# A two-layer graph network kernel: value products of two head pairs in one step, and row norms turned by rounded full-width products

## The chip, the cores and the metric

The kernel runs on one core of a Trainium2 chip. The metric is the device time of one execution in microseconds. Before the change it was 335.44 us, the median of 3 runs (334.61 to 335.58). All times of the profile come from one further, profiled execution of 335.22 us.

## The reference

625 nodes with 512 features each, 10,000 edges of 3 types. Layer 0 sums messages over the edges, and layer 1 is an attention with 8 heads of 64 over the same edges. Each layer normalises its input, clips it at zero, and its output is added to its input. The part around the change:

```
qkv = x @ W_qkv.T + b_qkv;  Q, K, V = split(qkv), each [nodes, 8, 64]
scores = einsum('ehd,ehd->eh', Q[receivers], K[senders]) / sqrt(64)
ex     = exp(scores - segment_max(scores)[receivers])
att    = ex / segment_sum(ex, receivers)[receivers]
msg    = segment_sum(att[:, :, None] * V[senders], receivers)
out    = msg.reshape(nodes, 512) @ W_ff.T + b_ff
```

## The kernel before

The kernel doesn't gather edges. In a first stage it counts them: one-hot rows made by VectorE and multiplied by TensorE give a dense table `adjT` of how many edges of each type run between two nodes. Layer 0 is then a set of dense products with that table (`z`, `gemm` units). For layer 1 the logarithm of the counts becomes a mask that is added to dense scores of 640 x 640 nodes (625, padded to five tiles of 128), so that the softmax over all nodes equals the one over the edges.

The attention is the last stage. It runs over five tiles of 128 receiving nodes and, in each, over 8 heads. Its steps are:

- `score` (TensorE, L1324): scores of one head of one tile, 128 x 640, in four products of 320 columns of rounded 32-bit numbers (F32R), a high and a low part of the keys. They go to two pairs of PSUM banks in turn, so a score step waits for the maximum of the step two before.
- `smax` (VectorE, L1019): adds the mask, copies to `s_sb` and takes the maximum.
- `exp` (ScalarE, L673): exponential into `p_sb`, with the row sums in `denom`.
- `turn` (TensorE, L1335): four transposes of 128 x 128 of `p_sb` into bank 5 or 6. `fill` copies them to `pT`, on ScalarE (L680) for even numbers and on VectorE (L1029) for odd ones. A `turn` waits for the `fill` two before.
- `pv` (TensorE, L1349): values times probabilities for one pair of heads, in bank 4: five blocks of nodes for each of two heads. A head has 64 values, so each product fills 64 partitions only, the even head the lower and the odd head the upper ones. The numbers are plain 32-bit, and each product appears in the trace as two instructions.
- `norm` (VectorE, L1036 and L1038): one over the row sums, [128 nodes, 8 heads], once a tile, when its last `exp` is done.
- `rb` (TensorE, L1359): the sums are per receiving node, but in bank 4 the node is the column. So the norm of each head is multiplied, broadcast to 64 columns, with the identity, which gives in bank 7 a 64 x 128 block with the norm of each column; eight products, again 64 partitions each. ScalarE copies bank 7 to `r_sb` (L687).
- `msg` (VectorE, L1048, then ScalarE L694 and GpSimd L497): bank 4 times `r_sb`, split in a high and a low part.
- `ff` (TensorE, L1369): the output product, four steps of three products of 512 columns, in bank 7; `out` (VectorE, L1055) adds the input, and a DMA stores the tile.

All engines run these steps in one order, the list `attention`: each step has a time in units of one head, from a few constants (`TURN`, `PV`, `RB`, `FF`), and the list is sorted by it. Each engine takes its own kinds of steps from it in that order; semaphores keep them together. In the steady state a `pv` step comes every two heads, `rb` comes between two `turn` and `score` steps of the next tile.

Of the kernel before, what the change touches and what calls it, by code (L numbers as in the profile page):

```python
# [26 lines left out]
F32 = mybir.dt.float32  # L27
F32R = mybir.dt.float32r
# [3 lines left out]
I32 = mybir.dt.int32  # L32
# [4 lines left out]
P = 128  # L37
# [5 lines left out]
def gnn_kernel(nc, x_d, src_d, dst_d, etype_d, ntype_d, wrel_d, brel_d, wself_d, bself_d,  # L43
# [28 lines left out]
    with ExitStack() as ctx:  # L72
        def sb(name, shape, dt):
            return ctx.enter_context(nc.sbuf_tensor(name, shape, dt))

        def sem(name):
            return ctx.enter_context(nc.semaphore(name))


        xs = sb("xs", [P, NT, D], F32)  # L80
        ident = sb("ident", [P, P], F32)
        ident16 = sb("ident16", [P, P], F16)
        bhl = sb("bhl", [BROWS, D], F32R)
        bv_rows = sb("bv_rows", [P, D], F32)
# [19 lines left out]
        tile_off = sb("tile_off", [1, 2, 8], F32)  # L104
        tile_off_i = sb("tile_off_i", [1, 8], I32)
        place_u = sb("place_u", [P, NT], U32)
        bounds = sb("bounds", [1, 3, 32], I32)
        bounds_f = sb("bounds_f", [1, 4, 32], F32)
        stats = sb("stats", [P, NT, 6], F32)
        mv = sb("mv", [P, 2, NT, 2], F32)  # L110
        rstd = sb("rstd", [P, 2, NT, 2], F32)
# [4 lines left out]
        neg_max = sb("neg_max", [P, NT, H], F32)  # L116
        denom = sb("denom", [P, NT, H], F32)
        recip = sb("recip", [P, 2, H], F32)
        norm = sb("norm", [P, 2, H], F32)


        Z_BYTES = 2 * KD * NP * 4
# [5 lines left out]
        def place(name, offset, shape, dt):  # L128
            return nc.alloc_sbuf_tensor_at(name, shape, dt, offset=arena0 + offset)
# [28 lines left out]
        edges_f = place("edges_f", o_r4 + 58752, [EC, 3, EL], F32)  # L158
        below = place("below", o_r4 + 60256, [P, P], F32)
        ones = place("ones", o_r4 + 60768, [P, P], F32)  # L160
        tile_iota = place("tile_iota", o_r4 + 61280, [P, 8], F32)
        full = place("full", o_r4 + 61312, [P, NT], F32)
        above = place("above", o_r4 + 61344, [P, T, NT], F32)
# [21 lines left out]
        sorted_d = nc.dram_tensor("sorted_rows", [SP, D], F32, kind="Internal").ap()  # L185
        self_d = nc.dram_tensor("self_rows", [SP, D], F32, kind="Internal").ap()

        banks = ctx.enter_context(nc.psum_tensor("banks", [P, 8, 512], F32))


        s_fill = sem("s_fill")
        s_edges = sem("s_edges")
        s_nodes = sem("s_nodes")
        s_x = sem("s_x")
# [130 lines left out]
        for f, at in enumerate(turn_at):  # L325
            placed += [(at, "turn", f), (at + 0.1, "fill", f)]
        pv_at = [turn_at[((2 * n + 2) * NT - 1) // 4] + PV for n in range(NT * KD)]
        placed += [(at, "pv", n) for n, at in enumerate(pv_at)]
        for it in range(NT):
            msg_at = max(pv_at[(it + 1) * KD - 1], it * H + RB) + 0.1  # L330
            placed += [((it + 1) * H, "norm", it), (it * H + RB, "rb", it)]
# [73 lines left out]
        def _(pool):  # L405
# [17 lines left out]
            nc.gpsimd.memset(edge_keys[:], 0.0).then_inc(s_fill, 1)  # L423
            pool.wait_ge(s_fill, 4)
            nc.gpsimd.tensor_copy(ident16[:], ident[:]).then_inc(s_fill, 1)
            nc.gpsimd.memset(zero_rows[:], 0.0).then_inc(s_fill, 1)
            nc.gpsimd.memset(ones[:], 1.0).then_inc(s_fill, 1)
            nc.gpsimd.memset(type_base[:], 0.0).then_inc(s_fill, 1)
# [269 lines left out]
        def _(dve):  # L698
# [311 lines left out]
            for step in attention:  # L1010
                kind, n = step
                if kind == "smax":
                    it, h = divmod(n, H)
                    dve.wait_ge(s_sc, n + 1)
                    dve.wait_ge(s_mask, 2 * (it + 1))
                    if n >= NS:
                        dve.wait_ge(s_exp, n - NS + 1)
                    c = 2 * (n % 2)
                    nc.vector.tensor_tensor_reduce(  # L1019
                        s_sb[:, n % NS, :].rearrange("p (a j) -> p a j", a=2), banks[:, c:c + 2, 0:HALF],  # L1020
                        mask_add[:, it, :].rearrange("p (a j) -> p a j", a=2), 1.0, 3.0e38, ALU.add, ALU.min,
                        neg_max[:, it, h:h + 1]).then_inc(s_smax, 1)
                    if n == 1:
                        split_q(KD - 1)
                elif kind == "fill" and n % 2 == 1:
                    dve.wait_ge(s_tr, n + 1)
                    if 4 * n + 3 >= NT * H:
                        dve.wait_ge(s_pv, (4 * n + 3 - NT * H) // (2 * NT) + 1)
                    nc.vector.tensor_copy(pT[:, 4 * n % (NT * H):4 * n % (NT * H) + 4, :],  # L1029
                                          banks[:, 5 + n % 2, :].rearrange("p (s i) -> p s i", s=4)  # L1030
                                          ).then_inc(s_ptd, 1)
                elif kind == "norm":
                    dve.wait_ge(s_exp, H * (n + 1))
                    if n >= 2:
                        dve.wait_ge(s_rb, n - 1)
                    chain(nc.vector.reciprocal(recip[:, n % 2, :], denom[:, n, :]))  # L1036

                    nc.vector.scalar_tensor_tensor(out=norm[:, n % 2, :], in0=neg_max[:, n, :], scalar=BIG / 2,  # L1038
                                                   in1=recip[:, n % 2, :], op0=ALU.is_lt, op1=ALU.mult
                                                   ).then_inc(s_norm, 1)  # L1040
                elif kind == "msg":
                    it, a = divmod(n, KD)
                    if a == 0:
                        dve.wait_ge(s_pv, KD * (it + 1))
                        dve.wait_ge(s_rsb, it + 1)
                    if it >= 1:
                        dve.wait_ge(s_mlo, n + 1 - KD)
                    nc.vector.tensor_tensor(msg_f[:, a], banks[:, 4, a * P:(a + 1) * P], r_sb[:, a],  # L1048
                                            ALU.mult).then_inc(s_msg, 1)
                elif kind == "out":  # L1050
                    dve.wait_ge(s_ff, n + 1)
                    dve.wait_ge(s_xb, n + 1)
                    if n >= 2:
                        dve.wait_ge(s_out[n % 2], 16 * (n // 2))
                    nc.vector.tensor_tensor(ybuf[:, n % 2, :], banks[:, 7, :], xs[:, n, :], ALU.add  # L1055
                                            ).then_inc(s_fin, 1)
# [3 lines left out]
        def _(pe):  # L1060
# [247 lines left out]
            for step in attention:  # L1308
# [18 lines left out]
                elif kind == "turn":  # L1327
                    pe.wait_ge(s_exp, (4 * n + 3) // NT + 1)
                    if n == 0:
                        pe.wait_ge(s_ufree, len(ring))  # L1330
                    if n >= 2:
                        pe.wait_ge(s_pta if n % 2 == 0 else s_ptd, n // 2)
                    for i in range(4):
                        h, jt = divmod(4 * n + i, NT)
                        ins = nc.tensor.transpose(banks[:, 5 + n % 2, i * P:(i + 1) * P],  # L1335
                                                  p_sb[:, h % NPR, jt * P:(jt + 1) * P], ident[:])
                    ins.then_inc(s_tr, 1)
                elif kind == "pv":
                    it, a = divmod(n, KD)
                    f = ((2 * n + 2) * NT - 1) // 4  # L1340
                    pe.wait_ge(s_pta, (f + 2) // 2)
                    pe.wait_ge(s_ptd, (f + 1) // 2)
                    if a == 0 and it >= 1:
                        pe.wait_ge(s_msg, KD * it)
                    for jt in range(NT):
                        for hh in range(2):
                            s = ((2 * n + hh) * NT + jt) % (NT * H)
                            h = 2 * a + hh
                            ins = mm(banks[64 * hh:64 * hh + 64, 4, a * P:(a + 1) * P],  # L1349
                                     v_sb[:, jt, h * DK:(h + 1) * DK], pT[:, s, :],  # L1350
                                     start=(jt == 0), stop=(jt == NT - 1), skip_group_check=True)
                    ins.then_inc(s_pv, 1)
                elif kind == "rb":
                    pe.wait_ge(s_norm, n + 1)
                    if n >= 1:
                        pe.wait_ge(s_fin, n)
                    for h in range(H):
                        me = 64 * (h % 2)
                        ins = mm(banks[me:me + 64, 7, h // 2 * P:(h // 2 + 1) * P],  # L1359
                                 norm[:, n % 2, h:h + 1].broadcast_to([P, DK]), ident[:],  # L1360
                                 start=(h < 2), stop=True, skip_group_check=True)
                    ins.then_inc(s_rb, 1)
                elif kind == "ff":
                    it, kt = divmod(n, KD)
                    pe.wait_ge(s_mlo, n + 1)
                    if kt == 0:
                        pe.wait_ge(s_rsb, it + 1)
                    for k, (pl, pw) in enumerate(PASSES):
                        ins = mm(banks[:, 7, :], msgT[:, it % 2, pl, kt, :], wffT[:, pw, kt, :],  # L1369
                                 start=(kt == 0 and k == 0), stop=(kt == KD - 1 and k == len(PASSES) - 1),  # L1370
                                 skip_group_check=True)
                    if kt == KD - 1:
                        ins.then_inc(s_ff, 1)
# [31 lines left out]
```

## Time and profile before

| | |
|---|---|
| median of 3 runs | 335.44 us (334.61 to 335.58) |
| profiled execution | 335.22 us, of which span 333.5 us |
| TensorE busy | 302.0 us (91%) |
| VectorE busy | 201.2 us (60%) |
| ScalarE busy | 143.0 us (43%) |
| GpSimd busy | 71.7 us (22%) |
| granted TensorE clock, mean | 0.974 |

The span is the time from the first to the last instruction; the execution has 1.7 us around it. The attention runs from about 234 us to the end. An engine that is busy for most of a stretch isn't shown to be the bound by that alone: the chain of waits, followed back from the last instruction, says which engine's work the end hangs on.

### The profile page before, as it was taken

Reading aid. Unit: us, or ns where it says so; the run is one execution under the profiler, and the core shown is the slowest. Engines: PE = TensorE matmul, PEld = TensorE weight load, DVE = VectorE, ACT = ScalarE, POOL = GpSimd, SP = SyncE. Lnnn points to the kernel's source line nnn. Section 1 sums busy time; section 2 is a strip of 40 time slices with the busy share of each in tenths; the row PEclk is TensorE's granted clock in tenths of the full one; section 3 lists DMA queues with packets and bytes.
Section 4 is the critical chain, followed back from the end, with each engine's and each line's share of the span. In section 5 each row is a group of like instructions: output and inputs, shape, how many; then the busy total and the mean of one; then the engine's idle time right before and its main releaser. Section 6 shows DMA issues by size and latency. Waiting matters only on the chain.

```text
span 333.5 us, 5488 instructions
## 1 busy us (share of the span) xinstructions
PE 302.0 (91%) x2006; PEld 228.6 (69%) x2006; DVE 201.2 (60%) x471; ACT 143.0 (43%) x282; POOL 71.7 (22%) x97
## 2 busy tenths in 40 slices
PE   2757699996699999999999999999799999999994
PEld 2512344442356778868788789999688888888883
DVE  5999944557794324434446962784976556565721
ACT  1155213236032332253342451677876466565721
POOL 6059500005840004470001330320001002020202
PEclk9999789998599999999999999999999999999999
DMA  5852894110740000003520000000000000000000
GB/s 173 281 186 100 267 392 154 38 64 33 253 152 13 2 1 3 2 2 128 149 103 2 0 0 3 0 2 1 0 2 0 34 2 2 32 2 33 1 33 28
DMA packets 10970, 22.29 MB, mean 67 GB/s; under 512 B 950, under 2 KB 966, under 8 KB 10938
## 3 DMA queue, kind: packets, MB, share of 16 engines
q1 hardware_dynamic: 8772, 16.80, 14.5%
q0 software_dynamic: 800, 2.62, 2.2%
q10 hardware_dynamic: 1366, 2.45, 2.1%
q8 instruction: 20, 0.33, 0.4%
q14 instruction: 12, 0.10, 0.1%
HBM read 15.60 MB, written 6.26 MB: 66 GB/s over the span
## 4 chain that ended last, share of the span: by engine, by line
PE 78%; DVE 14%; issue 2%; ACT 2%; DMA 2%; POOL 0%; DVEq 0%
PE banks L1260 13%; PE banks L1246 8%; PE banks L1206 8%; PE banks L1151 8%; PE banks L1349 7%; PE banks L1335 7%; PE banks L1324 7%; DVE key_hot L833 6%; PE banks L1099 6%; PE banks L1369 5%; DVE row_hot L840 3%; PE banks L1192 2%; DMA raw<-in_L_gnn_W_qkv_dram 2%; PE banks L1359 2%; PE banks L1236 1%
## 5 line engine op out<-in xcount | busy, mean ns | idle before, releaser
L1099 PE MATMUL banks<-key_hot,row_hot 128*128 128x480 f16 x120 | 35.8, 438 | 14.7 <-DVE key_hot L833 12.3
L1019 DVE CUSTOM_DVE_ANT_0 s_sb<-banks,mask_add 128x640 f32<-128x640 f32 x40 | 32.6, 822 | 22.2 <-PE banks L1324 22.1
L833 DVE TENSOR_SCALAR key_hot<-iota,picked 128x480 f16<-128x480 f16 x120 | 41.2, 410 | 0.0
L673 ACT ACTIVATE p_sb<-s_sb,neg_max 128x640 f32<-128x640 f32 x40 | 32.9, 823 | 17.3 <-DVE neg_max L1019 17.3
L1099 PEld LDWEIGHTS banks<-key_hot,row_hot 128*128 128x128 f16 x120 | 12.7, 108 | 36.8 <-DVE key_hot L833 15.7
L1206 PE MATMUL banks<-adjT,h 128*128 128x320 f16 x240 | 33.8, 299 | 0.6 <-DVE zT_even L892 0.6
L840 DVE TENSOR_TENSOR row_hot<-iota,picked_row 128x768 f16<-128x768 f16 x20 | 21.9, 1097 | 18.9 <-PE banks L1099 18.9
L1206 PEld LDWEIGHTS banks<-adjT,h 128*128 128x128 f16 x240 | 23.2, 98 | 10.4 <-DVE zT_even L892 1.2
L1335 PE MATMUL banks<-ident,p_sb 128*128 128x128 f32 x200 | 29.6, 275 | 0.2 <-ACT pT L680 0.2
L1260 PE MATMUL banks<-w_hl,zT_even 128*128 128x512 f32 x120 | 29.2, 394 | 0.0
L497 POOL TENSOR_TENSOR msgT<-msg_f,msgT 128x128 fp32r<-128x128 f32 x20 | 8.6, 460 | 95.7 <-ACT msgT L694 95.7
L1324 PE MATMUL banks<-k_hi,q_st 128*128 128x320 f32 x80 | 27.1, 348 | 2.0 <-DVE neg_max L1019 2.0
L1246 PE MATMUL banks<-h2T,wqkvT 128*128 128x320 f32 x192 | 28.3, 309 | 0.0
L1246 PEld LDWEIGHTS banks<-h2T,wqkvT 128*128 128x128 f32 x192 | 28.2, 188 | 0.1
L530 ACT ACTIVATE adjT<-banks 128x480 f16<-128x480 f32 x20 | 11.3, 570 | 37.2 <-PE banks L1099 37.1
L1151 PE MATMUL banks<-w_self,hsT 128*128 x56 | 26.7, 622 | 0.0
L1349 PE MATMUL banks<-pT,v_sb 128*64 128x128 f32 x400 | 26.0, 277 | 0.0
L1335 PEld LDWEIGHTS banks<-ident,p_sb 128*128 128x128 f32 x200 | 23.5, 141 | 3.0 <-issue 1.9
L1260 PEld LDWEIGHTS banks<-w_hl,zT_even 128*128 128x128 f32 x120 | 22.3, 188 | 4.4
L1349 PEld LDWEIGHTS banks<-pT,v_sb 128*64 128x64 f32 x400 | 21.5, 137 | 4.0 <-issue 3.8
L1324 PE MATMUL banks<-k_lo,q_st 128*128 128x320 f32 x80 | 24.0, 309 | 0.0
L446 POOL TENSOR_TENSOR w_hl<-raw,w_hl 128x512 fp32r<-128x512 f32 x12 | 15.0, 1284 | 41.5 <-ACT w_hl L521 41.5
(176 smaller groups left out, 473.3 us busy)
## 6 DMA issues: line engine op xcount, KB each, us to landing
w_self<-in_L_gnn_W_self_dram SPq DMA_DIRECT2D x3, 1024.0 KB, 9.4
raw<-in_L_gnn_W_rel_dram SPq DMA_DIRECT2D x3, 1024.0 KB, 14.6
raw<-in_L_gnn_W_qkv_dram SPq DMA_DIRECT2D x3, 1024.0 KB, 5.2
sorted_rows<-zero_rows ACTq DMA_DIRECT2D x1, 1792.0 KB, 10.9
self_rows<-hs SPq DMA_DIRECT2D x7, 256.0 KB, 2.0
hs<-sorted_rows SPq DMA_DIRECT2D x1, 1280.0 KB, 7.2
xs<-in_x_dram SPq DMA_DIRECT2D x1, 1024.0 KB
raw<-in_L_gnn_W_ff_dram SPq DMA_DIRECT2D x1, 1024.0 KB, 5.4
```

Of the source, the lines that this page charges most:

```text
L673: nc.scalar.activation(p_sb[:, n % NPR, :], s_sb[:, n % NS, :], ACT.Exp, scale=-1.0, bias=neg_max[:, it, h:h + 1], accum_out=denom[:, it, ...
L833: return nc.vector.tensor_scalar(to_key, iota[:], float(KEYS * w), key, ALU.add, ALU.is_equal)
L840: nc.vector.tensor_tensor(row_hot[:, par], iota[:, 0:P].unsqueeze(1).broadcast_to([P, G, P]), picked_row[:, w * G:(w + 1) * G].unsqueeze(2 ...
L1019: nc.vector.tensor_tensor_reduce(s_sb[:, n % NS, :].rearrange("p (a j) -> p a j", a=2), banks[:, c:c + 2, 0:HALF], mask_add[:, it, :].rear ...
L1099: mm(banks[:, w % 2, 0:KEYS], row_hot[:, w % 2, k, :], key_hot[:, w % 2, k, :], start=(k == 0), stop=True, skip_group_check=True).then_inc ...
L1151: ins = mm(pipe_bank(u), hsT[:, t % 4, kt, :], w_self[:, bass.ds(offsets[t] + kt * D, D)], start=(kt == 0), stop=(kt == KD - 1))
L1206: ins = mm(b[:, 0:HALF], h16[:, p, jt, feats], adj[:, jt, r, cols], start=(start and n == 0), stop=(stop and n == len(pick) - 1), skip_gro ...
L1246: ins = mm(b[:, 0:HALF], wqkvT[:, pw, kt, o:o + P], h2T[:, ph, kt, half * HALF:(half + 1) * HALF], start=(n == 0), stop=(n == 3 * KD - 1))
L1260: ins = mm(to, lhs[:, pl, kt, it * P:(it + 1) * P], weights[:, pw, kt, c0:c0 + cn], start=(start and n == 0), stop=(n == 3 * KD - 1), skip ...
L1324: ins = mm(banks[:, 2 * (n % 2) + half, 0:HALF], q_st[:, h, it * P:(it + 1) * P], k[:, h, cols], start=(p == 0), stop=(p == 1))
L1335: ins = nc.tensor.transpose(banks[:, 5 + n % 2, i * P:(i + 1) * P], p_sb[:, h % NPR, jt * P:(jt + 1) * P], ident[:])
L1349: ins = mm(banks[64 * hh:64 * hh + 64, 4, a * P:(a + 1) * P], v_sb[:, jt, h * DK:(h + 1) * DK], pT[:, s, :], start=(jt == 0), stop=(jt == ...
```

## The change

Two edits in the attention, and what they need.

The first sets the time of both `pv` steps of two neighbouring head pairs to that of the later one. The sort then puts them next to each other.

The second makes `rb` full width. VectorE now spreads the norm of each head over 64 columns itself, rounds this to F32R (`norm_hl[:, 0]`), and subtracts what was rounded from the exact one to have the rest (`norm_hl[:, 1]`). TensorE multiplies high and low parts of two heads together, 128 x 128, by an identity in F32R, eight products a tile, into the same places of bank 7. `norm_hl` has one buffer, so a `norm` step waits for the `rb` of the tile before. GpSimd makes the F32R identity at the start, and the small tables `bounds` are placed elsewhere.

```diff
+        ident_r = sb("ident_r", [P, P], F32R)
...
-        norm = sb("norm", [P, 2, H], F32)
+        norm = sb("norm", [P, H], F32)
...
+        norm_hl = place("norm_hl", o_r4 + 35328, [P, 2, H, DK], F32R)
...
-        placed += [(at, "pv", n) for n, at in enumerate(pv_at)]
+        placed += [(pv_at[n // 2 * 2 + 1], "pv", n) for n in range(NT * KD)]
...
             nc.gpsimd.tensor_copy(ident16[:], ident[:]).then_inc(s_fill, 1)
+            nc.gpsimd.tensor_copy(ident_r[:], ident[:]).then_inc(s_ident, 1)
...
-                    if n >= 2:
-                        dve.wait_ge(s_rb, n - 1)
+                    if n >= 1:
+                        dve.wait_ge(s_rb, n)
                     chain(nc.vector.reciprocal(recip[:, n % 2, :], denom[:, n, :]))
 
-                    nc.vector.scalar_tensor_tensor(out=norm[:, n % 2, :], in0=neg_max[:, n, :], scalar=BIG / 2,
-                                                   in1=recip[:, n % 2, :], op0=ALU.is_lt, op1=ALU.mult
-                                                   ).then_inc(s_norm, 1)
+                    chain(nc.vector.scalar_tensor_tensor(out=norm[:], in0=neg_max[:, n, :], scalar=BIG / 2,
+                                                         in1=recip[:, n % 2, :], op0=ALU.is_lt, op1=ALU.mult))
+                    spread = norm[:].unsqueeze(2).broadcast_to([P, H, DK])
+                    chain(nc.vector.tensor_copy(norm_hl[:, 0], spread))
+                    nc.vector.tensor_tensor(norm_hl[:, 1], spread, norm_hl[:, 0].bitcast(F32),
+                                            ALU.subtract).then_inc(s_norm, 1)
...
-                    for h in range(H):
-                        me = 64 * (h % 2)
-                        ins = mm(banks[me:me + 64, 7, h // 2 * P:(h // 2 + 1) * P],
-                                 norm[:, n % 2, h:h + 1].broadcast_to([P, DK]), ident[:],
-                                 start=(h < 2), stop=True, skip_group_check=True)
+                    if n == 0:
+                        pe.wait_ge(s_ident, 1)
+                    for a in range(KD):
+                        for p in range(2):
+                            ins = mm(banks[:, 7, a * P:(a + 1) * P],
+                                     norm_hl[:, p, 2 * a:2 * a + 2, :].rearrange("p h d -> p (h d)"),
+                                     ident_r[:], start=(a == 0 and p == 0), stop=(p == 1), skip_group_check=True)
```

TensorE, tile 0, from the transposes in front of the first `pv` step, before the change. L1335 are transposes, L1324 scores, L1349 value products:

```order
L1335 MATMUL banks<-ident,p_sb 128x128 x4
L1349 MATMUL banks<-pT,v_sb 64x128 x10
L1324 MATMUL banks<-k_hi,q_st 128x320
L1324 MATMUL banks<-k_lo,q_st 128x320
L1324 MATMUL banks<-k_hi,q_st 128x320
L1324 MATMUL banks<-k_lo,q_st 128x320
L1335 MATMUL banks<-ident,p_sb 128x128 x8
L1324 MATMUL banks<-k_hi,q_st 128x320
L1324 MATMUL banks<-k_lo,q_st 128x320
L1324 MATMUL banks<-k_hi,q_st 128x320
L1324 MATMUL banks<-k_lo,q_st 128x320
L1349 MATMUL banks<-pT,v_sb 64x128 x10
```

The same place after it (L1343 are the transposes, L1332 the scores, L1357 the value products):

```order
L1343 MATMUL banks<-ident,p_sb 128x128 x4
L1332 MATMUL banks<-k_hi,q_st 128x320
L1332 MATMUL banks<-k_lo,q_st 128x320
L1332 MATMUL banks<-k_hi,q_st 128x320
L1332 MATMUL banks<-k_lo,q_st 128x320
L1343 MATMUL banks<-ident,p_sb 128x128 x8
L1332 MATMUL banks<-k_hi,q_st 128x320
L1332 MATMUL banks<-k_lo,q_st 128x320
L1332 MATMUL banks<-k_hi,q_st 128x320
L1332 MATMUL banks<-k_lo,q_st 128x320
L1357 MATMUL banks<-pT,v_sb 64x128 x20
L1343 MATMUL banks<-ident,p_sb 128x128 x4
```

The first value step, which stood between transposes 5 and score 8, now stands behind score 9, joined with the second.

TensorE around the norm step of tile 3 (L1359), before:

```order
L1324 MATMUL banks<-k_lo,q_st 128x320
L1335 MATMUL banks<-ident,p_sb 128x128 x4
L1359 MATMUL banks<-ident,norm 64x128 x8
L1324 MATMUL banks<-k_hi,q_st 128x320
L1324 MATMUL banks<-k_lo,q_st 128x320
L1324 MATMUL banks<-k_hi,q_st 128x320
L1324 MATMUL banks<-k_lo,q_st 128x320
L1335 MATMUL banks<-ident,p_sb 128x128 x4
L1349 MATMUL banks<-pT,v_sb 64x128 x10
L1324 MATMUL banks<-k_hi,q_st 128x320
```

After (the norm step is L1369):

```order
L1332 MATMUL banks<-k_lo,q_st 128x320
L1343 MATMUL banks<-ident,p_sb 128x128 x4
L1369 MATMUL banks<-ident_r,norm_hl 128x128 x8
L1332 MATMUL banks<-k_hi,q_st 128x320
L1332 MATMUL banks<-k_lo,q_st 128x320
L1332 MATMUL banks<-k_hi,q_st 128x320
L1332 MATMUL banks<-k_lo,q_st 128x320
L1343 MATMUL banks<-ident,p_sb 128x128 x4
L1332 MATMUL banks<-k_hi,q_st 128x320
```

The value step that followed one score later has gone from here to the next pair, and the norm step has products of 128 rows of output.

VectorE, the norm step of tile 0 with the copy of transposes before it and the next maximum behind it, before:

```order
L1029 COPY pT<-banks 128x512
L1036 RECIPROCAL recip<-denom 128x8
L1038 SCALAR_TENSOR_TENSOR norm<-neg_max,recip 128x8
L1019 ISA s_sb,neg_max<-banks,mask_add 128x640
L1019 ISA neg_max 128x1
L1029 COPY pT<-banks 128x512
```

After:

```order
L1034 COPY pT<-banks 128x512
L1041 RECIPROCAL recip<-denom 128x8
L1043 SCALAR_TENSOR_TENSOR norm<-neg_max,recip 128x8
L1046 CAST norm_hl<-norm 128x512
L1047 TENSOR_TENSOR norm_hl<-norm,norm_hl 128x512
L1024 ISA s_sb,neg_max<-banks,mask_add 128x640
L1024 ISA neg_max 128x1
L1034 COPY pT<-banks 128x512
```

Two operations of 128 x 512 have come in ahead of the next maximum.

## Rows read from the trace of the kernel before

**Rows 1.** Page, chain that ended last: share of the span by engine.

```profile
PE 78%; DVE 14%; issue 2%; ACT 2%; DMA 2%; POOL 0%; DVEq 0%
```

**Rows 2.** Stretches, the attention: length; busy PE, PEld, DVE, ACT, POOL; clock; DMA.

```profile
240.00:326.00 86.00, 85.75 (x856) 74.61 (x854) 51.17 (x126) 49.62 (x117) 6.87 (x16) 1.00 0.04 14
```

**Rows 3.** Chain of waits in order of time: start us, us, what.

```profile
242.55 0.44 PE banks L1335 x4
...
245.89 0.59 PE banks L1324 x4
246.48 1.24 PE banks L1349 x20
247.72 0.59 PE banks L1335 x4
...
250.36 0.78 PE banks L1324 x4
...
258.95 0.70 PE banks L1369 x3
...
260.89 0.91 PE banks L1369 x3
...
268.08 1.02 PE banks L1359 x16
269.11 0.79 PE banks L1324 x4
...
323.57 2.21 PE banks L1349 x40
```

**Rows 4.** VectorE's groups by shape: count, busy us, mean ns, idle before.

```profile
L936 DVE CAST k_hi<-qk_f 64x640 fp32r<-64x640 f32 x8 | 5.3, 665 | 4.9 <-ACT qk_f L588 4.7
...
L999 DVE SCALAR_TENSOR_TENSOR xs<-self_sum,xs 128x512 f32<-128x512 f32 x5 | 3.5, 692 | 0.2
...
L946 DVE CAST k_lo<-k_lo 64x640 fp32r<-64x640 f32 x2 | 1.0, 490 | 0.1
...
L1038 DVE SCALAR_TENSOR_TENSOR norm<-neg_max,recip 128x8 f32<-128x8 f32 x5 | 0.8, 167 | 0.2
```

**Rows 5.** Timeline of TensorE's products behind value step 2: start us, us.

```profile
252.75 0.41 PE L1324 MATMUL banks<-k_hi,q_st 128*128 128x320 f32 x1
253.00 0.31 PE L1324 MATMUL banks<-k_lo,q_st 128*128 128x320 f32 x1
253.15 0.31 PE L1324 MATMUL banks<-k_hi,q_st 128*128 128x320 f32 x1
```

**Rows 6.** Timeline of TensorE's weight loads there, the second load.

```profile
252.85 0.19 PEld L1324 LDWEIGHTS banks<-k_lo,q_st 128*128 128x128 f32 x1
```

**Rows 7.** Timeline of VectorE around the norm steps of tiles 0, 1 and 4.

```profile
243.34 0.69 DVE L1029 COPY pT<-banks 128x512 f32<-128x512 f32 x1
244.46 0.20 DVE L1036 RECIPROCAL recip<-denom 128x8 f32<-128x8 f32 x1 [0.44 <-ACT p_sb L673]
...
245.05 0.82 DVE L1019 CUSTOM_DVE_ANT_0 s_sb<-banks,mask_add 128x640 f32<-128x640 f32 x1 [0.18 <-PE banks L1324]
...
260.78 0.17 DVE L1038 SCALAR_TENSOR_TENSOR norm<-neg_max,recip 128x8 f32<-128x8 f32 x1
262.42 0.82 DVE L1019 CUSTOM_DVE_ANT_0 s_sb<-banks,mask_add 128x640 f32<-128x640 f32 x1 [1.47 <-PE banks L1324]
...
319.88 0.69 DVE L1055 TENSOR_TENSOR ybuf<-banks,xs 128x512 f32<-128x512 f32 x1 [2.71 <-PE banks L1369]
```

**Rows 8.** Timeline of the start: GpSimd, ScalarE and TensorE around the identities.

```profile
3.91 0.34 POOL L425 CAST ident<-ident 128x128 f16<-128x128 f32 x1
...
6.22 0.20 ACT L536 ACTIVATE warm<-eps_c 128x1 f32<-128x1 f32 x1 [0.31 <-POOL sel L442]
...
8.45 0.47 ACTq L538 DMA_DIRECT2D sorted_rows<-zero_rows  x1
...
12.40 0.74 PEld L1105 LDWEIGHTS banks<-type_mask,below 128*128 128x128 f32 x2 [0.25 <-issue]
```

More of the change, by code:

```diff
@@ L106, in gnn_kernel @@
         place_u = sb("place_u", [P, NT], U32)
-        bounds = sb("bounds", [1, 3, 32], I32)
-        bounds_f = sb("bounds_f", [1, 4, 32], F32)
         stats = sb("stats", [P, NT, 6], F32)
@@ L160, in gnn_kernel @@
         ones = place("ones", o_r4 + 60768, [P, P], F32)
+        bounds = place("bounds", o_r4 + 64000, [1, 3, 32], I32)
+        bounds_f = place("bounds_f", o_r4 + 64384, [1, 4, 32], F32)
         tile_iota = place("tile_iota", o_r4 + 61280, [P, 8], F32)
@@ L186, in gnn_kernel @@
         self_d = nc.dram_tensor("self_rows", [SP, D], F32, kind="Internal").ap()
+        norm_hl = place("norm_hl", o_r4 + 35328, [P, 2, H, DK], F32R)
         banks = ctx.enter_context(nc.psum_tensor("banks", [P, 8, 512], F32))
         s_fill = sem("s_fill")
+        s_ident = sem("s_ident")
         s_edges = sem("s_edges")
```

## The prediction

> **What bounds the kernel now.** I read the chain of waits by engine first: 78% of the span hangs on TensorE, 14% on VectorE, nearly all of the latter in the adjacency stage at the start [rows 1]. Then the table by stretches: from 240 to 326 us TensorE is busy for 85.75 of 86.00 us, at a granted clock of 1.00 (2.4 GHz), while VectorE has 51 us and ScalarE 50 us of work [rows 2]. The edit changes nothing that is computed outside this stretch, which is the attention: its time is the sum of TensorE's steps. So I read the steps themselves off the chain of waits, where each piece runs from the end of the piece before to its own end [rows 3].
>
> Those rows show a cost that no instruction carries. Twenty value products (a step of one head pair, output on 64 partitions) take 1.24 us, but forty in one row take 2.21 us, so twenty cost 1.105 and about 0.14 is paid on the way in. What comes next is also longer than usual: a score step takes 0.78 us straight behind them and 0.59 elsewhere, a step of four transposes 0.59 against 0.44, an output step 0.91 against 0.70 [rows 3]. So every visit to the 64-wide form costs 0.14 us going in and 0.15 (transposes), 0.19 (scores) or 0.21 (output) coming out. The norm product is such a visit too: sixteen instructions in 1.02 us, which is 16 x 0.0553 = 0.885 plus 0.14 [rows 3].
>
> **The change, part by part.** *Pairing the value steps.* Before, a tile has four value steps and one norm step, each between full-width steps; for tiles 0 to 3 that makes 5 visits each, and for tile 4 there are 3, because the last norm step and two value steps already stand together: 23 visits. After, the value steps stand in twos and the norm step is full width: 2 visits per tile, 10 in all. 13 visits go. Nine of them were left into a score step (value steps 0, 2, 6, 10, 14 and norm steps 0 to 3), four into an output step (4, 8, 12, 16). 13 x 0.14 + 9 x 0.19 + 4 x 0.21 = 1.82 + 1.71 + 0.84 = 4.4 us off, all on TensorE, in a stretch where TensorE sets the time.
>
> *The norm products.* Out go, five times, sixteen instructions worth 0.885 us. In come eight rounded products of 128 x 128, with 128 columns moving. No row has a rounded product with so few columns, so I bound it. Above full speed it can't go: four score products of 320 columns take 0.59, 0.147 each, and three output products of 512 columns 0.70, 0.233 each [rows 3]; the line through both (0.45 ns a column) gives 0.061 us at 128 columns. But the weights have to be loaded, too. The first score product behind a visit is followed by the second after 0.25 us, the second by the third after 0.15 [rows 5]; the load in between is issued as soon as the first is through, 0.10 after it [rows 6]: a load of rounded weights that hides behind nothing costs 0.10 us. With 320 columns it hides; with 128 it doesn't fit under 0.061, so one product each 0.10 to 0.11 us is what I take, the same as one transpose now (0.44 / 4 [rows 3]). Eight make 0.87 us: no gain, no loss. Below: 0.061 each if the loads are quicker in a row, 8 x 0.061 = 0.49, 5 x 0.40 = 2.0 us less. Above: if moving and loading don't overlap, 0.16 to 0.17; if a short rounded product runs like an unrounded one, which takes two instructions of 0.109 (0.44 / 4 again, four transposes with 128 columns), 0.22; if its load isn't hidden either, 0.32.
>
> A rule that speaks against the cheap case: the Trainium skill, "TensorE: Matmul & The Clock Gate", Part 3, "The mechanism", says that a weight load overlaps with products in flight only where the row group differs. All of these products use all rows, so by the rule each would pay load and product one after the other. This trace doesn't agree for 320 columns: there the spacing is 0.147 us although every product has its own load of 0.10 [rows 5, 6]. For 128 columns no row decides, so it is a rival below.
>
> *Norms on VectorE.* Before, reciprocal and norm take 0.4 us with their link (0.20 and 0.167 [rows 4, 7]). In come a copy that spreads 8 values to 512 and rounds them, and a subtraction of 128 x 512. The copy's nearest rows are rounding casts of 64 x 640, 0.665 us and 0.490 [rows 4]; for 512 of 640 columns that is 0.39 to 0.53 us, with a broadcast read perhaps up to the 0.69 us of a 128 x 512 operation. The subtraction is of the size of L999, 0.69 us [rows 4]. I take 0.55 + 0.69 and two links of 0.03: 1.3 us more, five times (1.1 to 1.5). What hides it: in tile 1 VectorE waits 1.47 us behind the norm for the next scores, in tiles 2 and 3 the same, in tile 4 2.71 us for the output step [rows 7]. TensorE comes there earlier now by one value step and its visit, about 1.4 us, so up to 1.3 us of VectorE's work becomes late against it in tiles 1 to 3; but the maximum behind the norm is asked for only by the score step two later, behind output steps 2 and 3 of that tile, transposes and the value pair, over 4 us of TensorE's work. Nothing comes of it. In tile 0 the next score maximum begins 0.2 us behind the norm [rows 7], so it is late by 1.1 us, at about 246.1 instead of 245.05, and done at 247. Behind it on VectorE stand the copy of transposes 7 and the next maximum. TensorE asks for maximum 8 in score step 10, which now stands behind score 9, two value steps and transposes 8: at least 244.8 + 0.59 + 2.3 + 0.6 = 248.3. Slack 1.3 us: nothing. In the last tile the output sum behind the norm waits for TensorE longer than 1.3 us in any case. ScalarE's copy of the norms stays where it is, on an engine with 50 us of work in 86.
>
> *What is late next.* Where a value step went away, it had covered something. Transposes 7 wait for VectorE's copy of transposes 5, which began at 243.34 and ended at 244.03 [rows 7]. TensorE used to come there at about 245.4, 0.44 before the score step at 245.89 [rows 3]; now score 8, transposes 6 and transposes 7 follow the end of transposes 5 at 242.99 (242.55 + 0.44 [rows 3]) directly, so it arrives at about 243.7 and waits for 0.3 us. In later tiles the same place holds the norm step between score steps, and copies and exponentials are ahead by 0.2 us or more. Once, +0.3 us. The slots for transposed values: the first to be overwritten belongs to transposes 10, two transposes behind the moved pair; nothing.
>
> *At the start.* GpSimd copies the identity once more, about the 0.34 us of its fp16 copy, so that its last fill ends near 6.5 us instead of 6.2. ScalarE's next work behind it is the issue at 8.45, TensorE's first use 12.40 [rows 8]. Nothing. The bounds only lie elsewhere.
>
> **The sum.** -4.4 + 0.0 + 0.3 = -4.1 us. The profiled execution took 335.22 us (333.5 of span and 1.7 around it), so 331.1; the median of the runs is 0.2 higher, so 331.3.
>
> **The rivals.**
> Loads in a row are quicker (0.061 each): -6.1 us, 329.3. For it: the fit through 320 and 512 columns. Against: the 0.10 us of the bare load. Chance 0.06.
> Load and product don't overlap at 128 columns (0.165 each): eight take 1.32, 0.44 more than before, five times 2.2: 333.5. For it: a bare load is longer than the product, and no row shows how they share the array then. This is also what the skill's rule above would do. Chance 0.14.
> The gain is given back: short rounded products cost what unrounded ones cost (0.22). Eight take 1.76, 0.88 more, five times 4.4: the visits' saving is eaten, 335.7. For it: nothing in the trace shows that rounding is cheap below 320 columns, and 128-column products here all have 0.109 an instruction. Against: rounded products are one instruction, not two. Chance 0.20.
> Slower: the same, with the load of rounded weights bare each time (0.32): 2.56 a tile, 8.4 us more in all, minus 4.1: 339.7. It decides from 0.25 us a product on, where 5 x (2.0 - 0.885) = 5.6 us outweighs the saving by over 0.3%. Against: a product that long should hide a load of 0.10. Chance 0.08, with every other way to lose more than 1 us.
> That the pairs don't join (visits still paid inside a pair) I leave out: the last two value steps, already adjacent, run at 2.21 for forty [rows 3].
>
> **How the numbers follow.** My forecast has 0.52 and its own range is 330.2 to 332.1 (0.09 to 0.12 a product, waits of 0 to 0.6). Within 0.3% (1 us, what a measurement of this kernel can tell from no change) lies the third rival alone. Faster: 0.52 + 0.06 + 0.14 = 0.72; same 0.20; slower 0.08. The range for 8 in 10 goes from 330.2 to 335.8 and leaves out the first and the last rival, 0.14.
>
> **What would show it.** The chain after should have 2.3 us for each forty value products, ten of them, no value step of twenty, and score steps of 0.59 everywhere, behind the norm step too. The norm step should have eight instructions and take 0.87 us: 0.49 would be the first rival, 1.3 the second, 1.8 the third, 2.6 the fourth. VectorE should show 1.2 to 1.3 us for the two new operations and less idle time before the maxima, with TensorE still at about 81.5 us busy between 240 and 322. If TensorE shows idle time of over 1 us in the attention, a wait that I priced at 0.3 took the place of the visits and the forecast is wrong.

## The result and the profile after

The changed kernel takes 331.38 us (median of 4 runs, 331.32 to 331.60) against 335.51 us before: a ratio of 0.988 (95% interval 0.985 to 0.990), 4.1 us less. The forecast was 331.3.

The profiled execution took 331.60 us with a span of 329.9 us. That is only 3.6 us less than the one of before, because in it the attention began 0.5 us later. The stage itself is better measured by itself, from the start of the first score maximum to the start of the last output sum, on VectorE's timeline. Columns are start us, us and the instruction. Before:

```profile
233.50 0.82 DVE L1019 CUSTOM_DVE_ANT_0 s_sb<-banks,mask_add 128x640 f32<-128x640 f32 x1 [1.28 <-PE banks L1324]
...
330.11 0.69 DVE L1055 TENSOR_TENSOR ybuf<-banks,xs 128x512 f32<-128x512 f32 x1 [3.43 <-PE banks L1369]
```

After:

```profile
234.00 0.83 DVE L1024 CUSTOM_DVE_ANT_0 s_sb<-banks,mask_add 128x640 f32<-128x640 f32 x1 [1.28 <-PE banks L1332]
...
326.50 0.69 DVE L1063 TENSOR_TENSOR ybuf<-banks,xs 128x512 f32<-128x512 f32 x1 [3.41 <-PE banks L1379]
```

96.61 us before, 92.50 after: 4.11 us less. Below, "the stage" is this length. A second profile of the changed kernel had 92.49, so I read it to some hundredths, where whole runs tell about 1 us; no other kernel has a second profile.

The chain of waits after, from tile 0 into tile 1 and one period later, in the columns of [rows 3]. L1357 are value products, L1343 transposes, L1332 scores, L1379 output products and L1369 the norm step:

```profile
243.92 0.61 DVE pT L1034
244.54 0.14 issue
244.67 0.63 PE banks L1343 x4
245.31 0.58 PE banks L1332 x4
245.89 2.33 PE banks L1357 x40
248.22 0.59 PE banks L1343 x4
248.81 0.59 PE banks L1332 x4
249.41 0.44 PE banks L1343 x4
249.84 0.84 PE banks L1369 x8
250.68 0.64 PE banks L1332 x4
...
258.79 1.39 PE banks L1379 x6
...
267.57 0.84 PE banks L1369 x8
...
285.29 0.84 PE banks L1369 x8
```

Every value step is a block of forty in 2.33 us (2.36 for the last one, straight behind a norm step). The transposes behind such a block are still longer than their kind (0.59 for 0.44). The norm step takes 0.84 us instead of 1.02, and 0.64 instead of 0.78 for the scores behind it; six output products stand together in 1.39, where one value step used to split them in 0.70 and 0.91 [rows 3]. From one norm step to the next it is 17.72 us (285.29 - 267.57). The first three rows are the new wait: transposes 7 stand behind VectorE's copy of transposes 5, and they take 0.63 us instead of 0.44.

VectorE's norm step of tile 1, timeline, which answers to [rows 7]:

```profile
260.82 0.43 DVE L1046 CAST norm_hl<-norm 128x512 fp32r<-128x512 f32 x1
261.28 0.69 DVE L1047 TENSOR_TENSOR norm_hl<-norm,norm_hl 128x512 fp32r<-128x512 f32 x1
261.89 0.82 DVE L1024 CUSTOM_DVE_ANT_0 s_sb<-banks,mask_add 128x640 f32<-128x640 f32 x1
```

The 1.47 us of idle time ahead of the next maximum are gone: VectorE goes straight on. The stretches, for [rows 2], 86 us that begin 4 us earlier, as the stage now ends earlier:

```profile
236.00:322.00 86.00, 84.32 (x836) 77.58 (x834) 60.05 (x143) 53.56 (x126) 6.88 (x16) 1.00 0.04 14
```

VectorE has 60 us of work in it. TensorE has 1.7 us of idle time, of which 1.5 lie ahead of 240 us, where the kernel before has as much; from 240 to 322 us it is busy for 81.84 of 82.00 us, at the full clock.

### The profile page after: what moved, and what is told of

Its sections match the earlier page's. It is cut to its first block, busy times and chain, and to the rows that moved or that the text cites. A ratio compares the mean times of both kernels' runs of the same rounds, so it can differ in the third digit from the quotient of the medians.

```text
span 329.9 us, 5421 instructions
## 1 busy us (share of the span) xinstructions
PE 295.4 (90%) x1966; PEld 228.2 (69%) x1966; DVE 208.2 (63%) x481; ACT 143.7 (44%) x282; POOL 67.6 (21%) x98
## 4 chain that ended last, share of the span: by engine, by line
PE 77%; DVE 16%; ACT 3%; issue 2%; DMA 1%; POOL 0%; DVEq 0%
PE banks L1268 14%; PE banks L1214 9%; PE banks L1254 9%; PE banks L1159 7%; PE banks L1357 7%; PE banks L1343 6%; DVE key_hot L838 6%; PE banks L1332 6%; PE banks L1107 5%; PE banks L1379 4%; DVE row_hot L845 2%; PE banks L1244 2%; PE banks L1200 2%; PE banks L1369 1%; PE banks L1231 1%
## 5 line engine op out<-in xcount | busy, mean ns | idle before, releaser
L1107 PE MATMUL banks<-key_hot,row_hot 128*128 128x480 f16 x120 | 34.9, 427 | 16.8 <-DVE key_hot L838 13.0
L838 DVE TENSOR_SCALAR key_hot<-iota,picked 128x480 f16<-128x480 f16 x120 | 42.2, 417 | 0.0
L1343 PE MATMUL banks<-ident,p_sb 128*128 128x128 f32 x200 | 29.8, 275 | 0.3 <-ACT pT L685 0.2
L1332 PE MATMUL banks<-k_hi,q_st 128*128 128x320 f32 x80 | 26.8, 344 | 2.0 <-DVE neg_max L1024 2.0
L1343 PEld LDWEIGHTS banks<-ident,p_sb 128*128 128x128 f32 x200 | 23.5, 141 | 3.3 <-issue 2.3
L1159 PE MATMUL banks<-w_self,hsT 128*128 x56 | 25.5, 599 | 0.0
L1332 PE MATMUL banks<-k_lo,q_st 128*128 128x320 f32 x80 | 24.1, 309 | 0.0
L1357 PE MATMUL banks<-pT,v_sb 128*64 128x128 f32 x400 | 24.0, 275 | 0.0
L1357 PEld LDWEIGHTS banks<-pT,v_sb 128*64 128x64 f32 x400 | 21.6, 137 | 1.8 <-issue 1.7
```

Source lines behind the costliest of these rows:

```text
L838: return nc.vector.tensor_scalar(to_key, iota[:], float(KEYS * w), key, ALU.add, ALU.is_equal)
L1107: mm(banks[:, w % 2, 0:KEYS], row_hot[:, w % 2, k, :], key_hot[:, w % 2, k, :], start=(k == 0), stop=True, skip_group_check=True).then_inc ...
L1159: ins = mm(pipe_bank(u), hsT[:, t % 4, kt, :], w_self[:, bass.ds(offsets[t] + kt * D, D)], start=(kt == 0), stop=(kt == KD - 1))
L1332: ins = mm(banks[:, 2 * (n % 2) + half, 0:HALF], q_st[:, h, it * P:(it + 1) * P], k[:, h, cols], start=(p == 0), stop=(p == 1))
```

## The experiments

The theory: a change between products that fill 64 output partitions and full-width ones costs TensorE time on both sides; the change removes 13 of 23 visits to the narrow form, and the norm step in its new form costs what the old one did. The rivals: that only one of the two edits matters, that the price belongs to plain 32-bit numbers and not to the width, and that relief of other engines gave the time. All stage lengths, each from the same two rows of its kernel's profile. Where the last column says "one execution", there is only the profiled one, and the stage alone is compared:

| kernel | stage us | against the changed kernel | ratio of runs to before (95%) |
|---|---|---|---|
| before | 96.61 | +4.11 | |
| changed, again | 92.49 | -0.01 | 0.989 (0.986 to 0.991) |
| pairs only | 93.68 | +1.18 | 0.991 (0.989 to 0.993) |
| norm step only | 95.24 | +2.74 | 0.998 (0.996 to 0.999) |
| plain full-width norms | 92.54 | +0.04 | 0.988 (0.986 to 0.990) |
| 64 columns moved | 92.50 | 0.00 | one execution |
| 256 columns moved | 92.82 | +0.32 | one execution |
| norm products twice | 96.94 | +4.44 | one execution |
| narrow 16-bit norms | 90.81 | -1.69 | one execution |
| full-width 16-bit norms | 91.07 | -1.43 | 0.984 (0.981 to 0.987) |
| value steps in fours | 94.22 | +1.72 | 0.992 (0.989 to 0.994) |
| more VectorE work | 97.69 | +5.19 | one execution |
| 16-bit norms, later | 90.48 | -2.02 | 0.981 (0.979 to 0.983) |

**The changed kernel again.**

> The changed kernel once more, beside the others on the same chip: 4.1 us faster than before. It is the measure for the other three.

Median 330.51 us beside 334.73 of before: 4.2 us less.

**Pairs only.** The kernel before with

```diff
-        placed += [(at, "pv", n) for n, at in enumerate(pv_at)]
+        placed += [(pv_at[n // 2 * 2 + 1], "pv", n) for n in range(NT * KD)]
```

> The kernel before with the value steps paired and nothing else. Theory (a change between 64-wide and full-width products costs TensorE 0.14 us in and 0.15 to 0.21 us out): 9 visits go, 9 x 0.14 + 5 x 0.19 + 4 x 0.21 = 3.05 us, less one new wait of 0.3 us for the copy of transposes 5: 2.7 us faster than before, with TensorE's chain pieces of 2.33 us for forty value products and the norm steps unchanged at 1.02 and 0.78 behind. Rival (the time came from the norm step's new form, and pairing only moves work): 0 to 1 us faster.

The stage is 2.93 us shorter, the runs' medians 3.0 (331.72 against 334.73). The chain of waits (value products L1349, norm step L1359):

```profile
248.18 0.44 PE banks L1335 x4
248.61 1.02 PE banks L1359 x16
249.64 0.79 PE banks L1324 x4
```

The norm step is as it was, so the rival falls: most of the gain is the pairing's.

**Norm step only.** The changed kernel with that line the other way round.

> The changed kernel with the value steps back in their old places: only the norm step is full width. Theory: 4 visits go, 4 x (0.14 + 0.19) = 1.3 us, and the step itself is 0.84 us instead of 0.885, but 0.06 is lost in the scores behind it: 1.3 us faster than before, and the two parts add up to the whole (2.7 + 1.3 = 4.0). Rival (VectorE's 1.1 us more in every tile needs the room that pairing made): 0 to 0.5 us faster or slower, with new idle time on TensorE before score or transpose steps.

1.37 us shorter; medians 333.94 against 334.73. The medians differ by less than the stage, but the interval of their ratio, 0.2 to 1.5 us, holds it. TensorE has no wait that the kernel before didn't have, so VectorE's extra work fits without the pairing too.

The parts add to 4.30, 0.2 more than the whole. The chains of waits show where: from the norm step of tile 1 to that of tile 2 it is 18.74 us before, 18.01 with pairs only, 18.41 with the norm step only and 17.72 with both, so 1.02 us off where the parts give 1.06. It is much the same in each of the four such stretches, and lies in hundredths: six output products take 1.39 and 1.40 us with both edits, 1.38 and 1.39 with pairs only, and the scores are longer by as little. What makes them longer is open.

**Plain full-width norms.** VectorE spreads the norms exactly, TensorE multiplies them unsplit:

```diff
-                    chain(nc.vector.tensor_copy(norm_hl[:, 0], spread))
-                    nc.vector.tensor_tensor(norm_hl[:, 1], spread, norm_hl[:, 0].bitcast(F32),
-                                            ALU.subtract).then_inc(s_norm, 1)
+                    nc.vector.tensor_copy(norm_f[:], spread).then_inc(s_norm, 1)
...
                     for a in range(KD):
-                        for p in range(2):
-                            ins = mm(banks[:, 7, a * P:(a + 1) * P],
-                                     norm_hl[:, p, 2 * a:2 * a + 2, :].rearrange("p h d -> p (h d)"),
-                                     ident_r[:], start=(a == 0 and p == 0), stop=(p == 1), skip_group_check=True)
+                        ins = mm(banks[:, 7, a * P:(a + 1) * P],
+                                 norm_f[:, 2 * a:2 * a + 2, :].rearrange("p h d -> p (h d)"),
+                                 ident[:], start=(a == 0), stop=True, skip_group_check=True)
```

> The changed kernel with the norm step full width but in plain 32-bit numbers: VectorE spreads the norms exactly, without the low part, and TensorE issues four products (two instructions each) instead of eight rounded ones. Theory (a rounded product of 128 columns is bound by its weight load at 0.105 us, a plain instruction by its 128 columns at 0.109, and the width alone makes the visit): 8 x 0.109 = 0.87 us a step against 0.84 + 0.06 behind it, so the same time as the changed kernel within 0.3 us, with 0.6 us less VectorE work a tile. Rival (visits belong to plain 32-bit products, not to the width): the step and what is behind it show 0.14 and 0.19 again, 4 x 0.33 = 1.3 us slower than the changed kernel.

Chain of waits, the norm step (L1366) of tile 0 and the scores behind it:

```profile
249.14 0.89 PE banks L1366 x8
250.03 0.59 PE banks L1330 x4
```

No visit, though the numbers are the plain 32-bit ones of before: the width makes the price. (The weights of the old norm step were also read as a broadcast, which here they are not; but the value steps have no broadcast and paid the same 0.14 and 0.19.) The step's 0.89 is the changed kernel's 0.84 plus the 0.05 that there come out in the scores. So the split in high and low parts bought nothing; only the full width did. VectorE has one operation of 0.69 us less in each tile here, and the stage is no shorter: that work is hidden in the changed kernel. The medians say the same (330.96 and 330.51).

**64 and 256 columns.** The changed kernel's norm products with `ident_r[:, 0:64]`, and with `ident_r[:].unsqueeze(1).broadcast_to([P, 2, P])` into 256 columns.

> The changed kernel, but its eight norm products move only the first 64 columns of the identity (so only half of the norms are made). Theory (the weight load sets the pace of a short rounded product): spacing stays at 0.105 us, the norm step at about 0.84 us. Rival (2 cycles a column): 0.055 us each, the step 0.45 us.

> The changed kernel, but its norm products move 256 columns (the identity twice, into two neighbouring quarters of the bank, so that the sums are wrong). Theory (weight load of about 0.105 us beside 1 cycle a column): 256 columns take 0.107 to 0.12 us, the step 0.86 to 0.96 us and the score step behind it back at 0.59. Rival (2 cycles a column below some length): 0.21 us each, the step 1.7 us, the execution 4.4 us slower than the changed kernel.

Chain of waits, norm step and scores behind it, with 64 columns:

```profile
249.75 0.81 PE banks L1369 x8
250.56 0.67 PE banks L1332 x4
```

With 256:

```profile
248.70 0.95 PE banks L1369 x8
249.65 0.58 PE banks L1332 x4
```

With what is above 0.59 behind it counted in, a product costs (0.81 + 0.08) / 8 = 0.111 us with 64 columns, (0.84 + 0.05) / 8 = 0.111 with 128 and (0.95 - 0.01) / 8 = 0.118 with 256 (the other tiles have 0.95 to 0.97, up to 0.121). The time doesn't follow the columns; what is left is the weight load. The timeline of the changed kernel's weight loads fits that. Behind the norm step the second load of the scores starts 0.11 us after the first, though the product of the first moves 320 columns:

```profile
250.46 0.19 PEld L1332 LDWEIGHTS banks<-k_hi,q_st 128*128 128x128 f32 x1
250.57 0.19 PEld L1332 LDWEIGHTS banks<-k_lo,q_st 128*128 128x128 f32 x1
```

No run changes the load alone, so another fixed cost of a product of this type isn't excluded. The load would also explain the scores behind the step: their own load hides behind a norm product, and the fewer columns that has, the less it hides (0.08, 0.05, nothing). It would explain as well why the step with 64 columns was 0.03 us under the expected 0.84.

**Twice.** The same products issued again.

> The changed kernel with every norm step's eight products issued twice over. Theory (TensorE sets the time of the attention, and nothing else is near): 5 x 0.84 = 4.2 us more than the changed kernel, all of it in the norm step. Rival (other engines are close behind TensorE, so part of its work is free): clearly less than 4.2 us.

The norm piece is 1.74 us for sixteen, 0.90 more, and the stage 4.44 longer, against 5 x 0.90 = 4.5. All of it counts: TensorE is the bound, and eight products cost 0.90, not 0.84, once nothing of them is moved into the scores. So I don't take relief of another engine for the cause of the gain.

**Narrow 16-bit norms.** The step 64 wide again, with `norm16` and `ident16`.

> The changed kernel with the norm step 64-wide again but in 16-bit numbers (norms rounded to fp16, no low part: eight products of one instruction). Theory (the change of width costs, whatever the numbers): the step is short, but the visit is there: 0.1 to 0.15 us going in beyond its products, and 0.15 to 0.2 us more than 0.59 in the score step behind the norm. Rival (the price belongs to plain 32-bit products): score steps behind it take 0.59 to 0.65 as in the changed kernel.

Chain of waits, tile 1:

```profile
266.43 0.34 PE banks L1366 x8
266.78 0.79 PE banks L1329 x4
```

The scores behind it take 0.79 again, as behind the old narrow step. In the timeline the two products of a pair, one for each half of the partitions, start within 0.01 us of each other, and the pairs follow at 0.056; four pairs of that leave some 0.12 for going in. So 16-bit numbers pay the price of a visit too: it belongs to the width. The stage is shorter all the same, since 0.34 + 0.79 us stand where the changed kernel has 0.84 + 0.64: there is no low part, so there are eight half-width products in place of eight full-width ones, and they are of the quicker type.

**Full-width 16-bit norms**, high and low part in fp16, against the changed kernel:

```diff
-        norm_hl = place("norm_hl", o_r4 + 35328, [P, 2, H, DK], F32R)
+        norm16 = place("norm16", o_r4 + 35328, [P, 2, H, DK], F16)
...
-                                     norm_hl[:, p, 2 * a:2 * a + 2, :].rearrange("p h d -> p (h d)"),
-                                     ident_r[:], start=(a == 0 and p == 0), stop=(p == 1), skip_group_check=True)
+                                     norm16[:, p, 2 * a:2 * a + 2, :].rearrange("p h d -> p (h d)"),
+                                     ident16[:], start=(a == 0 and p == 0), stop=(p == 1), skip_group_check=True)
```

> The changed kernel with the norms in two 16-bit parts (fp16 high and low, and the fp16 identity) instead of two rounded 32-bit parts; still eight full-width products a tile. Theory (a rounded product of 128 columns is paced by its weight load, 0.112 us; the width alone makes the visit): a 16-bit product is paced by its 128 columns, about 0.055 us as in the 64-wide 16-bit step, so the norm step takes 0.45 us instead of 0.84 and the score step behind it stays at 0.59 to 0.65: 5 x 0.4 = 2 us faster than the changed kernel, perhaps 0.1 a tile less where transposes begin to wait for copies. Rival (0.11 us is what any full-width load costs): no faster than the changed kernel.

Chain of waits, tile 1:

```profile
265.55 0.45 PE banks L1368 x8
266.00 0.65 PE banks L1331 x4
266.64 0.44 PE banks L1342 x4
267.08 0.59 PE banks L1331 x4
267.67 1.01 PE banks L1342 x8
```

The step is 0.45 us, 0.39 less; in the timeline its weight loads are 0.10 us long, those of the rounded numbers 0.19. But the stage is only 1.43 shorter, not 5 x 0.39 = 1.95: eight transposes take 1.01 us, where they had 0.87, in four tiles. TensorE is early by so much that the second four wait for ScalarE's copy, which stands behind its copy of the norms and ends at 267.91 us; TensorE's next weight load starts at 268.02. Median 329.48 against 334.95.

**Value steps in fours.** `pv_at[n // 4 * 4 + 3]` for all four, and a ring of 56 slots.

> The changed kernel with all four value steps of a tile in one, behind the last of them; the ring of transposed blocks has 56 slots instead of 40, so that nothing waits for a slot. Theory (a value step is also the cover under which VectorE and ScalarE catch up): 5 more visits go, 5 x 0.29 = 1.5 us, but in tile 0 score step 10 then comes 1.3 us before maximum 8, which stands behind the norms on VectorE, and the transposes of each tile wait some tenths for copies, 3 to 4 us in all: 2 us slower than the changed kernel. Rival (only visits count): 1.5 us faster.

1.72 us longer than the changed kernel. The chain of waits in tile 0 shows where (value products L1363 come later; L1052 and L1053 are VectorE's norm operations):

```profile
243.63 0.44 DVE norm_hl L1052
...
244.70 0.82 DVE s_sb L1030
245.52 0.02 DVE neg_max L1030
245.54 0.04 issue
245.58 0.85 PE banks L1338 x4
```

Score 10 waits for maximum 8, which stands behind the norms on VectorE: 1.03 us of idle time on TensorE by the timeline, which the first pair had covered. In the last tile the timeline has another wait, for VectorE's copy of transposes:

```profile
316.12 0.63 PE L1349 MATMUL banks<-ident,p_sb 128*128 128x128 f32 x4 [0.60 <-DVE pT L1040]
```

Counted from the end of one tile's last value block to that of the next, tile 0 is 1.6 us longer than in the changed kernel, tiles 1 to 3 are 0.12 us shorter each, and the rest is 0.5 longer. Merging all narrow steps saves 5 visits and uncovers more than they cost.

**More VectorE work.** Four more subtractions in each norm step.

> The changed kernel with VectorE's subtraction of the norms made five times instead of once, 4 x 0.63 = 2.5 us more VectorE work a tile, 12.6 us in all. Theory (slack of about 1.3 us behind the norm in tile 0, more in the others): tile 0 gives 1.2 us of idle TensorE before score step 10 and some tenths at transposes 10 and 12, the later tiles 0.2 us each: 2 to 3.5 us slower than the changed kernel. Rival (VectorE is hidden wholly): no change; other rival (VectorE's work counts in full): 12 us slower.

5.19 us longer: VectorE isn't hidden wholly, and its work doesn't count in full (20 x 0.72 = 14.4 us), but my 2 to 3.5 was too low. Up to the end of its last value pair, tile 0 is 2.3 us longer, where I had 1.2 and some tenths; tiles 1 to 3 are 0.6 longer each, where I had 0.2; the rest is 1.1 longer. The chain of waits shows what I left out, in tile 2:

```profile
276.05 0.30 DVE msg_f L1059
276.36 0.02 issue
276.38 0.62 ACT msgT L699 x3
...
280.24 0.21 DVE recip L1041
...
280.48 0.18 DVE norm L1043
...
281.15 0.70 DVE norm_hl L1048
```

From the messages on, the chain leaves TensorE for ScalarE's exponentials and VectorE's norm step, here and in tile 3.

**16-bit norms, later.** `RB` 11.4 instead of 10.8.

> The kernel with norms in two 16-bit parts, its norm step moved one score and one transpose step later (RB 11.4 instead of 10.8), so that ScalarE copies the transposes in front of it before it copies the norms. Theory (in the 16-bit version the second of two adjacent transpose steps waits 0.14 us in every tile for ScalarE's copy, which stands behind the copy of the norms): that wait goes in tiles 0 to 3, the piece of eight transposes is 0.87 us again instead of 1.01, and the attention is 0.5 us shorter than with the step in its old place. Rival (the wait is for the exponential or for VectorE): the piece stays at 1.0 us and nothing is gained.

Chain of waits, tile 1:

```profile
266.36 0.45 PE banks L1368 x8
266.81 0.65 PE banks L1331 x4
267.45 0.87 PE banks L1342 x8
```

The wait is gone, the stage is 0.59 us shorter (4 x 0.14 = 0.56). At 328.65 us (334.88 before, on the same chip) this is the fastest version, 1.9% under before.

## Why the prediction was right

*The price of a visit and their number.* 13 visits, 4.4 us. The pairing took 2.93 us where the same prices and the one wait give 2.75, the norm step 1.37 where 4 visits give 1.32. The prices were a little too low: twice 1.24 against 2.33 is 0.15 for going in, and 0.70 + 0.91 [rows 3] against the 1.38 of six output products that stand together in the same chain is 0.23 for coming out into them, where the prediction had 0.14 and 0.21. The mechanism, that the width makes the price, was tested apart from the type of the numbers and held both ways. The Trainium skill, "TensorEngine Tiling (Array Packing)", "Tiling Modes", says that a change of tiling mode drains TensorE, and the traces fit that, in that each such change costs time: about 0.14 us in, 0.15 to 0.23 out. They show the price and not the drain itself.

*The norm products at no gain and no loss.* This was the open price, 0.49 to 2.6 us a step. It came to 0.84, with 0.05 more in the scores behind it: 0.89 against 0.885. The reason fits too: the columns don't set the pace, and a load of about 0.11 us would. The prediction had read 0.10 us for a bare load off [rows 5] and [rows 6]; the row there shows a load that is 0.19 long and starts 0.10 behind the first product, so 0.10 is the distance of two starts and not a length. The rule that I set against it (a load overlaps only with products in other rows) would have made it 0.16 or more; at 0.111 this trace doesn't agree with it for 128 columns either. Of "what would show it", the busy time of TensorE came out (81.84 us for 81.5, with 0.16 us idle from 240 us on); one detail was wrong, as I expected 0.59 behind the norm step, and it is 0.64.

*VectorE hidden.* 0.43 + 0.69 us with the links between dependent operations, 1.2 a tile, where I took 1.3. It is hidden in the changed kernel; the overload shows that this isn't so at 2.9 us more.

*What is late next.* Transposes 7 wait for the copy of transposes 5, as forecast, but the working of that wait was wrong. It let TensorE arrive at 243.7 us; the rows give 242.99 + 0.59 + 0.44 = 244.02, just when the copy ends (244.03), so by them there is next to nothing to wait. What the trace after shows is the way from the copy's end to TensorE's start, 0.14 us, and a first piece of 0.63 us instead of 0.44: 0.33 together, of which the timeline calls 0.16 idle. The 0.3 in the sum was right by luck. In effect tile 0's first removed visit gains nothing: the value pair ends at the same distance from the start of the stage as the second value step did, 248.22 - 234.00 = 14.22 us, before 247.72 - 233.50 = 14.22 [rows 3].

The sum was 4.1 and the stage shows 4.11. Some of that is luck: the parts measured alone gave 0.2 us more than the prediction had for them (4.30 against 4.1), and together they gave 0.2 less than alone. That the median came within 0.1 us of 331.3 is luck also, since the same kernel had 330.51 in the second set of runs.

What stays open is why the attention begins at other times, between 231.46 and 234.00 us in these profiles, although nothing ahead of it that counts was changed. The two profiles of the changed kernel differ by 2.5 us there, and by 2.4 already at 46 us; in the first 50 us the granted clock was 0.97 in one and 1.00 in the other, but no run shows whether that is the cause. It makes the medians less sharp than the stage.

## What to carry to other kernels

Read the same kind of step off the chain of waits in several surroundings: where it is longer behind one neighbour, the difference is a price that no instruction carries, and reordering removes it. Before merging steps, ask what each of them covered, since the step that leaves a gap was also the time in which other engines caught up. Where a short product's time doesn't fall with its columns, as here with rounded 32-bit numbers, fewer columns gain nothing, but a shorter type may: fp16 took half.

## What the runs showed of the hardware

At the full clock, with 128 x 128 weights: a rounded 32-bit product took 0.111 us with 64 or 128 columns moved and 0.118 to 0.121 with 256; a plain 32-bit one two instructions of 0.111; an fp16 one 0.056 to 0.062 ((0.45 + 0.05) / 8). Splitting a 32-bit operand in two rounded parts to avoid the plain form therefore gains nothing at 128 columns; two fp16 parts nearly halve the time. The prediction had no row for a rounded product of so few columns, nor for an fp16 one. Two narrow instructions, one on each half of the output partitions, start within 0.01 us of each other, and a pair takes about what one full-width instruction does (0.109 us against 0.111 plain, 0.056 for both in fp16): narrow steps lose at their ends and not in between. VectorE's cast from a broadcast read, 128 x 512, took 0.43 us, within the estimate of 0.39 to 0.53 that the prediction scaled from casts of 64 x 640 without a broadcast.
